# A recurrent-attention and mixture-of-experts block on one core: four groups of 512-column matmuls issued as halves of 256 columns, with a new table of steps for all token operations

## What is computed

```
xn = ln(ln(layernorm(x)));  x1 = the inner ln
r, k, v, g, decay, a = projections of xn and of xn shifted by one token   (128x128 and low rank)
for each token t:                                  # the scan, 512 steps, state 16x16x8x8
    sa    = state . a_t
    state = state * d_t + sa * b_t + v_t * k_t
    out_t = state . r_t
x2 = x1 + (groupnorm(out) + bonus) * g @ W_o
kf = ln(x2) mixed with its shift
y1 = x + x2 + square(relu(kf @ W_ffn1)) @ W_ffn2   (128 -> 512 -> 128)
h  = layernorm(y1);  expert = argmax(h @ W_router)  (4 experts)
y  = gelu(h @ W1[expert] + b1[expert]) @ Wo + bo + h
result = y1 + layernorm(y) * gamma + beta
```

## Time and profile before

| what | us |
|---|---|
| median of 3 runs | 1217.58 |
| the profiled execution | 1216.56 |
| its span | 1214.7 |
| TensorE busy | 1043.4 (86%) |
| VectorE busy | 890.9 (73%) |
| ScalarE busy | 668.6 (55%) |
| GpSimd busy | 629.7 (52%) |

### The profile page before, as it was taken

One profiled execution on the slowest core, in us unless ns is written; L12 is line 12 of the kernel. 1 busy time (PEld: TensorE's weight loads), 2 busy tenths in 40 slices (PEclk: granted clock), 3 DMA queues, 4 the chain that ended last, 5 costly groups with the idle time before them and its releaser, 6 DMA issues.

```text
span 1214.7 us, 17920 instructions
## 1 busy us (share of the span) xinstructions
PE 1043.4 (86%) x5395; PEld 566.0 (47%) x5395; DVE 890.9 (73%) x2283; ACT 668.6 (55%) x1093; POOL 629.7 (52%) x885
## 2 busy tenths in 40 slices
PE   3666689989898989989898989999798989888866
PEld 2343354455454455455454555455454545454432
DVE  4567777887878787877878787887878787876220
ACT  2634464847475565747475665847475565734331
...
DMA packets 62759, 41.88 MB, mean 34 GB/s; under 512 B 7100, under 2 KB 56252, under 8 KB 62536
## 3 DMA queue, kind: packets, MB, share of 16 engines
...
...
## 4 chain that ended last, share of the span: by engine, by line
PE 58%; DVE 14%; ACT 13%; issue 7%; DMA 4%; SPq 3%; ACTq 0%; DVEq 0%
PE fin_a L514 9%; PE fin_b L514 9%; PE sa_ps L359 9%; PE pre_a L298 6%; PE mid_ps L468 5%; PE fin_b L523 3%; DVE state L857 3%; SPq L262 3%; DMA rs_f<-row_ers 3%; PE mid_ps L298 3%; DVE upd L853 3%; PE vb_ps L338 3%; ACT hid L718 2%; DVE s_a L843 2%; ACT L548 2%
## 5 line engine op out<-in xcount | busy, mean ns | idle before, releaser
L1030 POOL TENSOR_TENSOR plus_kv<-state,kv 128x128 f32<-128x128 f32 x512 | 284.7, 556 | 418.5 <-DVE state L857 393.3
L359 PEld LDWEIGHTS sa_ps<-s_a,con 128*128 128x128 f32 x1024 | 183.6, 201 | 307.2 <-DVE s_a L843 230.3
L359 PE MATMUL sa_ps<-s_a,con 128*128 128x128 f32 x1024 | 237.5, 316 | 76.0 <-DVE s_a L843 75.9
L853 DVE TENSOR_TENSOR upd<-sa_ps,b_t 128x128 f32<-128x128 f32 x512 | 147.8, 289 | 169.5 <-PE sa_ps L359 164.8
L1022 POOL TENSOR_TENSOR s_r<-state,r_t 128x256 f32<-128x256 f32 x256 | 219.1, 856 | 1.3 <-DVE state L857 1.3
L857 DVE TENSOR_TENSOR state<-upd,plus_kv 128x128 f32<-128x128 f32 x512 | 175.2, 342 | 18.0
L843 DVE TENSOR_TENSOR s_a<-state,a_t 128x128 f32<-128x128 f32 x512 | 149.4, 292 | 18.5
L548 ACT ACT_TABLE_LOAD x101 | 129.6, 1283 | 1.8
L514 PE MATMUL fin_b<-h_e,mat 128*128 128x512 f32 x256 | 128.2, 616 | 0.8 <-ACT pick L733 0.8
L514 PE MATMUL fin_a<-h_e,mat 128*128 128x512 f32 x256 | 122.1, 593 | 0.0
L830 DVE TENSOR_TENSOR kv<-vb_ps,k_t 128x512 f32<-128x512 f32 x128 | 87.5, 684 | 0.3 <-issue 0.2
...
## 6 DMA issues: line engine op xcount, KB each, us to landing
rs_p<-row_rs SPq DMA_DIRECT2D x128, 64.0 KB, 2.1
...
```

The source lines that it names most:

```text
L359: mm(sa_ps[:, 0:STATE], k("sum8"), s_a[:], start=True, stop=True).then_inc(s["sa"], 1)
L853: tt(ib(upd[:]), ib(sa_ps[:, 0:STATE]), over_i(b_t[c.slot][:, t * B:(t + 1) * B]), ALU.mult).then_inc(s["upd"], 1)
L1030: tt(plus_kv[:, (t % 2) * STATE:(t % 2 + 1) * STATE], st(t), kv[:, at:at + STATE], ALU.add).then_inc(s["plus_kv"], 1)
```

## The change

Every matmul of `f1`, `f2`, `moe` and `mo` is issued as two matmuls of 256 columns over the same weights and the same bank, each with its own entry in the table. The semaphores are raised as before, by the last one of a bank. The bias matmul L517 stays whole. The waits are the same, for both halves. The table of all token operations is another one; the number of operations other than these matmuls is the same. The core of the diff:

```diff
-    "hid": (50, 51, 53, 56), "kf": 51, "d_frs": 51, "f1": (52, 52, 53, 54), "f2": (55, 56, 57, 57),
+    "hid": (52, 53, 54, 55), "f1": (52, 52, 52, 53, 53, 54, 54, 55), "f2": (55, 55, 56, 56, 56, 57, 57, 57),
...
-    "moe": (68, 68, 70, 70, 70, 71, 71, 72, 73, 76, 76, 77, 78, 78, 79, 79), "act": (70, 71, 77, 77),
+    "moe": (68, 68, 68, 69, 70, 70, 70, 70, 70, 70, 71, 71, 71, 72, 72, 72, 73, 73, 76, 76, 76, 77, 77, 77, 78, 78, 78, 79, 79, 79, 79, 79),
...
+            def half(part):
+                return slice(part * COLS // 2, (part + 1) * COLS // 2)
...
                 for j in range(J):
-                    if at == AT["f2"][j]:
-                        pe.wait_ge(s["hid"], c.count(max(j + 1, 3), J))
-                        last = mm(mid_ps[:], w("ffn2", j), hid[j][:], start=(j == 0), stop=(j == J - 1))
-                        if j == J - 1:
-                            last.then_inc(s["f2"], 1)
+                    for part in range(2):
+                        if at == AT["f2"][2 * j + part]:
+                            pe.wait_ge(s["hid"], c.count(max(j + 1, 3), J))
+                            last = mm(mid_ps[:, half(part)], w("ffn2", j), hid[j][:, half(part)],
+                                      start=(j == 0 and part == 0), stop=(j == J - 1), skip_group_check=True)
+                            if j == J - 1 and part:
+                                last.then_inc(s["f2"], 1)
```

More of the change, by code:

```diff
@@ L33 @@
-    "rec": -4, "rkb_ps": -4, "r_t": -3, "b_t": -3, "a_t": -2, "g2": -2, "th_g": -1, "bonus": 0, "gate": 0,
-    "bonus_b": 23, "x_res": 34, "gj": 37, "gsq": 37, "grs": 38, "gxh": 39, "gaff": 39, "gg": 39, "wo": 41,
-    "x2": 42, "fsq": 42, "fc": 43, "x2x": 43, "frs": 44, "fj": 45, "xf": 46, "fxh": 48,
-    "hid": (50, 51, 53, 56), "kf": 51, "d_frs": 51, "f1": (52, 52, 53, 54), "f2": (55, 56, 57, 57),
-    "d_ers": 57, "y1": 58, "ec": 58, "ej": 58, "esq": 59, "h": 61, "router": 61, "ers": 62, "best": 62,
@@ L38 @@
-    "onehot": 63, "masks": 63, "h_e": (65, 66, 69, 70), "pick": 66, "pick_sb": 66,
-    "moe": (68, 68, 70, 70, 70, 71, 71, 72, 73, 76, 76, 77, 78, 78, 79, 79), "act": (70, 71, 77, 77),
-    "y1b": 78, "mo": (80, 80, 81, 82), "lsq": 84, "y2": 85, "lrs": 85, "lj": 86, "d_lrs": 86, "store": 89,
-    "lxh": 91, "res": 91,
+    "c0": -32, "j0": -30, "sq0": -28, "x_in": -25, "rs0": -23, "xh0": -23, "d_rs0": -23, "d_rs1": -23,
+    "c1": -22, "x1": -21, "sq1": -21, "rs1": -21, "j1": -21, "xn": -18, "xh1": -17, "wa": -16, "dx": -16,
@@ new lines @@
+    "mix_k": -15, "k": -15, "mix_g": -15, "th_w": -15, "mix_r": -15, "mix_v": -14, "w2": -14, "kks": -13,
+    "key": -12, "th_d": -12, "rk": -12, "v": -11, "k2": -11, "d_rk": -11, "val_tm": -10, "g1": -10, "cum": -9,
+    "p": -9, "val": -8, "val_sb": -8, "k_t": -7, "kk": -7, "r": -6, "kki": -6, "rkb": -5, "rec": -4,
+    "rkb_ps": -4, "r_t": -3, "b_t": -3, "a_t": -2, "g2": -2, "th_g": -2, "gate": -2, "bonus": 0,
+    "bonus_b": 26, "gj": 37, "x_res": 38, "gsq": 39, "gxh": 39, "gaff": 39, "gg": 39, "grs": 41, "wo": 41,
@@ new lines @@
+    "x2": 42, "fsq": 43, "fc": 43, "x2x": 43, "frs": 45, "fj": 45, "xf": 48, "fxh": 48, "d_frs": 48, "kf": 51,
+    "hid": (52, 53, 54, 55), "f1": (52, 52, 52, 53, 53, 54, 54, 55), "f2": (55, 55, 56, 56, 56, 57, 57, 57),
+    "d_ers": 58, "y1": 58, "ec": 58, "ej": 58, "esq": 58, "h": 61, "router": 61, "ers": 61, "best": 63,
+    "onehot": 63, "masks": 63, "h_e": (65, 66, 69, 70), "pick": 66, "pick_sb": 68,
+    "moe": (68, 68, 68, 69, 70, 70, 70, 70, 70, 70, 71, 71, 71, 72, 72, 72, 73, 73, 76, 76, 76, 77, 77, 77, 78, 78, 78, 79, 79, 79, 79, 79),
@@ L42 @@
+    "y1b": 73, "act": (74, 74, 77, 79), "mo": (79, 80, 80, 80, 81, 81, 82, 83), "lsq": 84, "y2": 85,
+    "lrs": 86, "lj": 86, "d_lrs": 89, "lxh": 90, "res": 90, "store": 93,
 }
@@ new lines, in work @@
+                for j in range(J):
+                    for part in range(2):
+                        if at == AT["mo"][2 * j + part]:
+                            pe.wait_ge(s["act"], c.count(max(j + 1, 3), J))
+                            last = mm(fin_b[:, half(part)], w("Wo", j), act_j[j][:, half(part)],
+                                      start=(j == 0 and part == 0), stop=(j == J - 1), skip_group_check=True)
+                            if j == J - 1 and part:
+                                last.then_inc(s["mo"], 1)
```

58 lines of the change are left out of this document (27 added, 31 removed).

## The result

The change takes 1221.64 us, the median of 20 runs (1217.10 to 1227.38); the kernel before, run beside it, 1218.41 (20 runs, 1214.51 to 1222.26). The ratio is 1.0033, with an interval of 1.0019 to 1.0048. The forecast was 1213.0, in a range of 1203 to 1224: the time lies in the range, on the side opposite to the forecast. The profiled execution of the change took 1221.53 us and has a span of 1219.7, 5.0 over that of before.

What follows compares the result with a forecast made beforehand. No engine is full: waits of `upd` for TensorE and chains across engines bound the kernel. 14 x (-0.75 + 0.25) = -7.0, plus 2.5 for the clock, gives -4.5 and a median of 1213.0, range 1203 to 1224.

Steps and rivals of the forecast that it cites:

- The row DMAs from exponential to `h`: End of the chain from `y1`: four row DMAs, with `h` starting 4.1 us after the exponential, read from chunk 8.
- the clock: More idle TensorE time before the router's matmul: half clock reaches step 0 in two or three more chunks, +2.5 us.
- the first chunk and the tail: First chunk's preparation and tail after the last scan: chains of waits whose order hardly changes, put at 0.
- 4-11: Steps 4 to 11: step 5 falls to 1.52 for 1.93, steps 7 to 9 within 0.03; together -0.43 a chunk.
- 12-18: Steps 12 to 18: step 13 falls by 0.42, step 16 grows by 0.70; together -0.10 a chunk.
- 19-29: Steps 19 to 29, set by chains rather than load: step 24 takes 2.08 for 1.52; together -0.15 a chunk.
- 30-1: Steps 30 to 1: `best` in step 31 makes steps 30 and 31 4.15 for 4.56; together -0.07 a chunk.
- more passes: TensorE's 56 extra half passes: a pair costs 0.007 more than one of 512 columns; +0.25 a chunk.
- some 1.6 longer: Step 26 grows by this many us as `kki`, `lxh` and `res` move there; step 27 more than 2 us shorter.
- the cover is gone and the gain with it: Step 29: `h`, with only `ec` some 0.15 earlier, holds the step, so moving work to step 26 gains little.
- The 0.34 given back in step 0: Step 0: expert masks start 0.1 later and stand 0.5 in front of the scan matmul, costing 0.34 a chunk.
- That rival: Steps 28 to 1: half clock lasts longer, another 1.1 in each chunk, +13, or +5 in half; 1223 to 1230; chance 0.19.

Runs made afterwards that it cites:

- i_warm_old5: The kernel before (old table, whole matmuls) with five added TensorE matmuls a chunk to hold the clock, none in step 1: 1206.08 us, ratio 0.9897.
- j_split_old2: The kernel before with its old table, all 28 matmuls split, both halves in the whole's step; a_split_old run again for a profile: 1226.23 us beside 1219.70.
- f_phase0: The change with the 18 pairs that stand in one step issued whole, plus five added TensorE matmuls a chunk: 1200.85 us, ratio 0.9860.
- a_split_old: The kernel before with its old table, every one of the 28 matmuls split, both halves in the step of the whole: 1224.56 us, ratio 1.0048.
- b_whole_new: The change's new table with whole matmuls, each in the step of its first half: 1224.80 us, ratio 1.0049.

## Why the prediction was wrong

The step of the prediction that failed is what it took as fixed or small outside the step sums. The row DMAs from exponential to `h` were a constant 4.1 and are not (+3.6 us over the steady chunks, put at nothing); the clock was given +2.5 and took +4.9; and the first chunk and the tail were put at 0 and took +5.0. The sums over the steps, whose total was near, could not make up for that.

**The steps: the total right to 0.15, in part by errors that cancel.** An undisturbed chunk of the change takes 66.84, one of before 67.49: -0.65, where the prediction had -0.75 + 0.25 = -0.50. By its own stretches:

| stretch | forecast | measured |
|---|---|---|
| 4-11 | -0.43 | -0.30 |
| 12-18 | -0.10 | +0.05 |
| 19-29 | -0.15 | -0.09 |
| 30-1 | -0.07 | -0.31 |
| more passes | +0.25 | 0.11, and within the rows above |

Steps 5 and 13 are 1.52, as forecast, step 15 1.52 (1.66 before), step 16 3.04 (3.0 forecast), step 17 3.23. In 4 to 11 the miss is steps 7 to 9, 0.12 longer in all where 0.03 was allowed; in 12 to 18 it is step 14, 2.29 for 2.14. Within 19 to 29 step 24 was to take 2.08 and takes 1.73, while step 23 takes 2.50 for 2.08 before. In 30 to 1 the -0.31 is steps 30 and 31 alone (4.26 for 4.56), and 0.3 is what the old table loses to the half clock in step 31, as i_warm_old5 shows; with the clock held both tables take 4.25 there in most chunks. VectorE in chunk 9: steps 21 and 22, 26 to 28, `h`:

```profile
705.97 0.79 DVE L870 TENSOR_TENSOR state<-upd,plus_kv 128x128 f32<-128x128 f32 x1
706.79 0.29 DVE L856 TENSOR_TENSOR s_a<-state,a_t 128x128 f32<-128x128 f32 x1
...
714.92 0.29 DVE L856 TENSOR_TENSOR s_a<-state,a_t 128x128 f32<-128x128 f32 x1
715.13 0.94 DVE L918 SCALAR_TENSOR_TENSOR mix_g<-mix_v,half_kk,dec_bt 128x512 f32<-128x512 f32 x1
715.99 0.68 DVE L963 TENSOR_TENSOR y<-mid_ps,x2x 128x512 f32<-128x512 f32 x1
...
717.30 1.06 DVE L1011 SCALAR_TENSOR_TENSOR res<-y,vec,y1b 128x512 f32<-128x512 f32 x1
...
718.93 0.29 DVE L856 TENSOR_TENSOR s_a<-state,a_t 128x128 f32<-128x128 f32 x1
720.95 0.29 DVE L856 TENSOR_TENSOR s_a<-state,a_t 128x128 f32<-128x128 f32 x1
...
723.97 0.69 DVE L968 TENSOR_TENSOR h<-fin_a,rs_f 128x512 f32<-128x512 f32 x1 [0.35 <-DMA rs_f<-row_ers]
```

GpSimd beside it:

```profile
705.34 1.27 POOL L1057 TENSOR_TENSOR k<-key,k 128x512 f32<-128x512 f32 x1
...
716.64 1.19 POOL L1069 TENSOR_SCALAR bonus<-bonus,vec 128x512 f32<-128x512 f32 x1
```

In step 21 `state` took 0.79 in place of 0.29 while GpSimd's `k2` ran from 705.34 to 706.61, and the step stays at 2.02. In step 26 `kki` came first and took 0.94 (0.74 before), and `res` took 1.06 beside `bonus_b` (0.75 before); the four operations stand in one step, which is 4.01 for 1.94 before. The prediction had it "some 1.6 longer", from durations alone: it is 2.1 longer, and step 27 2.2 shorter (2.02 for 4.26). From `y1` on the chain is as described: `h` starts 723.97 - 700.21 = 23.76 after step 19, where 23.85 or 0.15 less was named. That `h` would hold step 29, "the cover is gone and the gain with it", was right: with nothing late it is 0.11 longer than before. The 0.34 given back in step 0 did not come: it takes 1.59 in both at full clock.

**"More passes": mis-sized.** TensorE in chunk 9 of the change, steps 6 and 7 (start us, us, instruction):

```profile
672.81 1.89 PE L525 MATMUL fin_b<-h_e,mat 128*128 128x256 f32 x8
674.54 0.38 PE L528 MATMUL fin_b<-pick,b_all 68*128 68x512 bf16 x1
674.76 1.03 PE L525 MATMUL fin_a<-h_e,mat 128*128 128x256 f32 x4
```

Eight half passes start within 674.54 - 672.81 = 1.73, where four whole ones took 1.72, and in j_split_old2 56 more passes cost 0.11 a chunk, 0.002 each. The prediction took 0.007 from a straight line between eight passes of 128 columns and one of 512; the 0.005 by which 0.1125 exceeds a quarter of 0.430 is found only in passes as short as that; half passes don't pay it. The Trainium skill (TensorE: Matmul & The Clock Gate, "Wait — 56ns, not 53.3ns?") has 2.5 ns for each, by which the term would have been 0.14 a chunk, an estimate; the 0.11 measured agrees with it.

**"Clock": the sign right, the size half.** Forecast: two or three more chunks of the long kind, +2.5. Measured: steps 0 to 3 are 0.38 longer in the mean, 13 x 0.38 = 4.9, above the 4.4 that it gave as the upper end. The reason given for the sign holds in part: TensorE's idle time before the router's matmul did grow, from 1.3 to 1.4 in the chunks with nothing late. But with a late `h` it is 2.0 to 2.8, and there the clock was back in step 0 in five of six. The count of long chunks rose by one only, from 7 to 8 (the prediction had 9 from the mean, as it put the late `h` of chunk 11 down to the clock too). The rest is a third kind that the forecast had left to a rival: in chunks 5 and 10 the clock was at half through steps 0 to 3, 8.7 for 6.16. That rival named the place and the mark rightly, but put it into half or all of the chunks.

**The missing term.** "From `y1` to `h` goes a chain over ... four row DMAs, and `h` ... 4.1 after the exponential" was read from one chunk and taken as a constant. It is a constant only where no packet of instructions comes in between. The trace of before had the case: VectorE in chunk 11, and the queues between exponential and `h`, 852.90 to 858.40.

```profile
858.47 0.69 DVE L955 TENSOR_TENSOR h<-fin_a,rs_f 128x512 f32<-128x512 f32 x1 [1.69 <-DMA rs_f<-row_ers]
```

```profile
q1 hardware_dynamic: 729, 0.55, 38.1%
q8 instruction: 1, 0.02, 1.1%
```

That `h` is 1.45 late, but the prediction looked only at chunk 8. With 17% more TensorE instructions there are more packets, and they fall on 7 `h` for 1. In step 29 of the steady chunks that is 5.1 us for 1.45 before, +3.6; the other 1.5 of 13 x 0.39 = 5.1 is the hold by `h` that was foreseen.

**"The first chunk's preparation and the tail: 0."** Measured +5.0, of which chunk 1 has 2.0 (steps 0 to 3 8.20 for 6.16: the clock once more), the tail 1.5, about 0.7 of it one late `h`. The head's 0.5 and chunk 0's 1.0 were not traced to a cause; in f_phase0, with the same table, chunk 0 is 62.80, so that they may be particular to one execution.

The sum against the profiled spans: -10.1 from the stretches without step 29, +1.5 for `h` holding that step (together -8.6, forecast -7.0), +4.9 clock, +3.6 late rows, +5.0 ends: +4.9, where 1219.7 - 1214.7 = 5.0. Against the medians the change loses 3.2; the profile of before lies 1.9 under its median of 20 runs. So the sum that was reasoned from load and waits held, and two things outside it did not: the clock after the gap before `h`, and DMA queues that also carry code. That the time still lies in the range was given by the room left for the rivals.

**What stays open.** a_split_old and b_whole_new are both 0.5% slower than before, and single profiles scatter by up to 7 us around the medians; j_split_old2 shows the parts for one execution, not how they would average. What decides between the three kinds of steps 0 to 3 (6.15, 7.4, 8.7) in otherwise equal chunks is not shown. Why packets at nearly the same distance delay `h` by 0.4 in one chunk and by 1.4 in another is not settled either.
